# Six row loads for the third attention, issued one a tile early in the routed experts instead of together near their end

## The chip, the cores and the metric

One Trainium2 chip, one core of it. The metric is the device time of one launch in microseconds, as the median of several executions. In the profile PE is TensorE, PEld its weight loads, DVE VectorE, ACT ScalarE, POOL GpSimd, SP SyncE; SPq and POOLq are the queues on which SP and POOL issue DMAs.

## What is computed

A batch of 32 sequences of 128 rows by 256 features goes through two attentions against the context and two feed-forward blocks, each on the layer-normed input with a residual added:

```python
x = x + _L0_xattn_ref(_layernorm(x, axis=-1), ctx_1024, ctx_1024)      # 16 heads
x = x + _L0_ffn_ref(_layernorm(x, axis=-1), ...)                        # 8 experts, top 2, plus a shared one
x = x + _L1_xattn_ref(_layernorm(x, axis=-1), ctx_1024, ...)            # c2q and q2c attention, 4*D -> D
x = x + _L1_ffn_ref(_layernorm(x, axis=-1), ...)                        # butterfly, gelu, butterfly
```

The part around the change is the second line. In it each row is sent to two of eight experts:

```python
h = jnp.einsum('bsd,edh->bseh', x, W1) * jax.nn.silu(jnp.einsum('bsd,edh->bseh', x, W3))
expert_out = jnp.einsum('bseh,ehd->bsed', h, W2)
out = jnp.einsum('bsed,bse->bsd', expert_out, w_full)
out = out + jnp.einsum('bsh,hd->bsd', hs, Ws2)
```

## The kernel before

The kernel runs in blocks, one after the other with a barrier of all engines between them: the first attention (to about 230 us of the trace), the shared expert with routing (to about 383), the routed experts (to about 711), the "third attention" (the reference's third line, to about 890) and the last feed-forward. There is no scheduler: each engine has its own program, a Python loop over tiles whose order is written out by hand, and waits on semaphores.

**Shared expert.** In pairs p of sequences the sum of the residual and the shared expert's output is stored from `ao` to `acc_d` in HBM (L708, semaphores `s_ast`). POOL scatters the normed rows, sorted by expert, to `xs_d`.

**Routed experts.** The sorted rows are worked through in NE = 71 tiles of 128 rows, t = 0 to 70. For a tile PE multiplies its turned rows `xT` with the expert's weights W3 into `Ge` and W1 into `Ue`, six matmuls each; ACT makes `sg` of `Ge`, DVE makes `he` of both. `he` has to be turned before it meets W2. In tiles 0 to 31 and in the last two PE turns it (L1075). In tiles 32 to 68 (`by_dma`) ACT and DVE split it into two halves `hs` (L1145, L1183), and a transposing DMA on SP's queue writes `hT` (L1048). PE's product `Ye` of tile t - 2 comes at the end of loop step t (L1082 is the line of all three products, in a helper). DVE scales it to `ye`, and SP stores that to `ys_d`.

**SP's queue.** It does this in step t, in this order: load `xe` for tile t + 4 (once PE has turned tile t), transpose tile t in the `by_dma` tiles (once `hs` is there), store `ye` of tile t - 2. In step 8 seven small loads come first (`small_weights`, L1027 to L1030). In step NE - 6 = 65 six loads of 256 KB come first: `ax` (the stored `acc_d`, L1039) and `cx` (the context, L1040) for the pairs 0, 1 and 2 of the third attention, behind a wait for all stores of `acc_d`. `ax` and `cx` have buffers of their own, which nobody writes or reads before.

**POOL** multiplies out the butterflies of the last block beside it, with loads of 1 MB (`bw`, L1232).

**Third attention.** POOL gathers each row's two expert outputs from `ys_d` (L1414) once all `ye` are stored. DVE adds them to `ax`, norms the sum, and PE turns it (`Tc`, L1762) and the context (`Tq` from `cx`, L1765). The pairs from 3 on are loaded in that block (L1388, L1392), with waits on pairs three before.

Of the kernel before, what the change touches and what calls it, by code (L numbers as in the profile page):

```python
# [56 lines left out]
def build_program(nc, x, ctx_in, Wr, rb, W1, W2, W3, Ws1, Ws2, Ws3, w_cq, b_cq, w_c, b_c, w_q, b_q,  # L57
# [12 lines left out]
    NE = (NB * TOPK * P + E * (P - 1)) // P  # L70
# [8 lines left out]
    def dram(name, shape, dt=F32):  # L79
        return nc.dram_tensor(name, shape, dt, kind="Internal").ap()  # L80
# [4 lines left out]
    acc_d = dram("acc_d", (NB, P, D))  # L85
# [4 lines left out]
    with ctx:  # L90
# [874 lines left out]
        ax = per("ax", [P, 3, 2, D])  # L965
        cx = per("cx", [P, 3, 2, D])
        s_w5, s_b5 = sem("s_w5"), sem("s_b5")
        s_ax, s_cx = sems("s_ax", 3), sems("s_cx", 3)
# [6 lines left out]
        with ExitStack() as ph:  # L975
# [24 lines left out]
            pair = lambda a, p: a[2 * p:2 * p + 2, :, :].rearrange("t p n -> p t n")  # L1000
# [17 lines left out]
            with nc.Block() as block:  # L1018
                @block.sync
                def _(sp):  # L1020
                    as_col = lambda a: a.rearrange("(c p) -> p c", p=P)
                    as_rows = lambda a, n: a.rearrange("(o d) -> o d", o=1).broadcast_to([P, n])

                    def small_weights():

                        for i, w in enumerate((w_cq, w_q, w_c)):
                            sp.dma_start(wcq[:, i, :], as_col(w), allow_slow_non_contiguous=True).then_inc(s_w5, 16)  # L1027
                        sp.dma_start(blb[:, :], as_rows(b_l, D)).then_inc(s_w5, 16)
                        for i, b in enumerate((b_cq, b_c, b_q)):
                            sp.dma_start(bias3[:, i:i + 1], as_rows(b, 1)).then_inc(s_w5, 16)  # L1030

                    for t in range(-2, NE + 2):
                        if t == 8:
                            small_weights()
                        if t == NE - 6:
                            for j in range(2):
                                sp.wait_ge(s_ast[j], 16 * (NP // 2))
                            for p in range(3):
                                sp.dma_start(ax[:, p, :, :], pair(acc_d, p)).then_inc(s_ax[p], 16)  # L1039
                                sp.dma_start(cx[:, p, :, :], pair(ctx_in, p)).then_inc(s_cx[p], 16)  # L1040
                        if t + 4 < NE:
                            if t >= 2:
                                sp.wait_ge(s_xt, t + 1)
                            sp.dma_start(xe[:, t % 4, :], xs_d[(t + 4) * P:(t + 5) * P, :]).then_inc(s_xe[t % 4], 16)
                        if by_dma(t):
                            sp.wait_ge(s_hl4, BASE_L + t + 1)
                            sp.wait_ge(s_ye, t - 2)
                            sp.dma_start_transpose(hT[:, t % 3, :, :, :].rearrange("p l c n -> p (l c) n"),  # L1048
                                                   hs[:, t % 2, :, :].rearrange("p l n -> p (l n)")).then_inc(s_hT[t % 2], 16)
                        if t >= 2:  # L1050
                            sp.wait_ge(s_yc, t - 1)
                            sp.dma_start(ys_d[(t - 2) * P:(t - 1) * P, :], ye[:, t % 2, :]).then_inc(s_yst[t % 2], 16)
# [278 lines left out]
        with ExitStack() as ph:  # L1331
# [48 lines left out]
            pair = lambda a, p: a[2 * p:2 * p + 2, :, :].rearrange("t p n -> p t n")  # L1380
# [656 lines left out]
```

## Time and profile before

| | |
|---|---|
| median of 3 runs | 1049.26 us (1045.29 to 1050.29) |
| span of the profiled execution | 1070.0 us |
| PE busy | 977.7 us (91%) |
| DVE busy | 708.4 us (66%) |
| ACT, POOL busy | 558.5 us, 558.9 us (52% each) |
| SP's DMA queue (q1) | 111.60 MB, 35.8% of 16 engines |

Of the profiled execution only the span is known, no time of its own beside it; its span is 20.7 us above the median of the runs. PE's busy share says little by itself, since stages with different limits are put together in it. The granted clock (PEclk) is 1.00 at 2.4 GHz and 0.50 at 1.2 GHz.

### The profile page before, as it was taken

To read this page: it belongs to the slowest core of one execution; us is meant where nothing else is said; L and a number is where in the kernel's file an instruction comes from. 1 tells how busy PE (TensorE), PEld (TensorE's weight loads), DVE (VectorE), ACT (ScalarE), POOL (GpSimd) and SP (SyncE) were. 2 spreads that over 40 slices of the span, in tenths; PEclk is the share of its full clock that TensorE was granted. 3 is DMA by queue.
4 is the path that set the end of the run, shared out by engine and by line. 5 is a ranking of instruction groups with operands and counts; after the bars stand their busy time and mean duration, and the time that the engine had idled before them with its cause. 6 is when DMAs were issued, how large, how long until landed. Compare 5 with 4: busy or idle time off the path is not lost. (4 is left out here: it accounts for less than half of the span.)

```text
span 1070.0 us, 27041 instructions
## 1 busy us (share of the span) xinstructions
PE 977.7 (91%) x9282; PEld 757.6 (71%) x9282; DVE 708.4 (66%) x1682; ACT 558.5 (52%) x1140; POOL 558.9 (52%) x737
## 2 busy tenths in 40 slices
PE   5999999767699989999999999877999998999998
PEld 3666666556388856666666666546989997989897
DVE  6999999756366734445455555457888975565653
ACT  5999999723154523333323333335445546667664
POOL 6777777204544549999999990227556501000000
PEclk9999999979699999999999999988999999999999
DMA  5455444346599874555445555724454302211110
GB/s 147 156 163 161 151 155 141 100 153 197 180 296 318 284 212 155 187 174 177 139 93 121 122 117 118 177 79 129 127 155 142 120 31 70 61 41 60 39 50 30
DMA packets 153161, 147.90 MB, mean 138 GB/s; under 512 B 51440, under 2 KB 141776, under 8 KB 151248
## 3 DMA queue, kind: packets, MB, share of 16 engines
q1 hardware_dynamic: 143808, 111.60, 35.8%
q0 software_dynamic: 9232, 34.67, 9.8%
q8 instruction: 78, 1.28, 0.5%
q14 instruction: 43, 0.35, 0.1%
HBM read 84.22 MB, written 52.30 MB: 128 GB/s over the span
## 5 line engine op out<-in xcount | busy, mean ns | idle before, releaser
L941 POOL DMA_INDIRECT xs_d<-ht,slot x64 | 67.0, 1048 | 86.5 <-DMA ht<-h_d 40.3
L1082 PE MATMUL Ye<-wm,hT 128*128 x852 | 105.9, 274 | 2.7 <-DMA hT<-hs 2.5
L1082 PE MATMUL Ge<-wm,xT 128*128 x426 | 104.3, 381 | 2.1 <-issue 1.0
L1082 PE MATMUL Ue<-wm,xT 128*128 x426 | 103.5, 379 | 0.0
L1082 PEld LDWEIGHTS Ye<-wm,hT 128*128 128x128 f16 x852 | 83.6, 98 | 27.3 <-issue 3.5
L1943 ACT ACTIVATE gf<-H,bup,wdesc 128x256 f32<-128x256 f32 x128 | 71.8, 563 | 54.1 <-DVE g L1916 33.9
L1972 PE MATMUL H<-T6s,wm 128*128 128x256 f16 x768 | 94.0, 273 | 2.7 <-PEq L1381 1.6
L1984 PE MATMUL Y<-wm,g 128*128 128x256 f16 x768 | 93.8, 273 | 1.5 <-DVE g L1916 1.5
L1414 POOL DMA_INDIRECT yg<-ys_d,slot x64 | 66.8, 1044 | 51.8 <-DMA ys_d<-ye 34.4
L1916 DVE SCALAR_TENSOR_TENSOR g<-gf,g 128x512 f16<-128x512 f32 x64 | 44.7, 698 | 71.0 <-ACT g L1948 71.0
L1150 ACT ACTIVATE sg<-Ge 128x512 f32<-128x512 f32 x71 | 42.4, 597 | 82.8 <-PE Ge L1082 82.8
L350 DVE TENSOR_REDUCE nmx<-S 128x8 bf16<-128x1024 f32 x64 | 78.4, 1224 | 9.9 <-PE S L532 7.1
L1972 PEld LDWEIGHTS H<-T6s,wm 128*128 128x128 f16 x768 | 75.0, 98 | 12.0 <-issue 1.9
L1984 PEld LDWEIGHTS Y<-wm,g 128*128 128x128 f16 x768 | 75.0, 98 | 10.5 <-DVE g L1916 2.1
L1187 DVE SCALAR_TENSOR_TENSOR xT<-XB,xT 128x256 f16<-128x256 f32 x71 | 30.1, 424 | 71.8 <-ACT xT L1156 71.8
L1082 PEld LDWEIGHTS Ge<-wm,xT 128*128 128x128 f16 x426 | 41.9, 98 | 38.0 <-issue 3.9
L1856 POOL TENSOR_TENSOR rs<-mv,epsc 128x2 f32<-128x2 f32 x14 | 3.2, 226 | 125.3 <-DVE mv L1880 125.3
L429 ACT ACTIVATE pT<-ST 128x1024 f32<-128x1024 f32 x64 | 68.0, 1062 | 1.0 <-PE ST L564 0.9
L1082 PEld LDWEIGHTS Ue<-wm,xT 128*128 128x128 f16 x426 | 41.7, 98 | 34.5
L1140 ACT CAST hT<-HT 128x512 f16<-128x512 f32 x34 | 19.9, 585 | 80.8 <-PE HT L1075 80.8
L1194 DVE SCALAR_TENSOR_TENSOR he<-Ue,sg 128x512 f32<-128x512 f32 x71 | 49.1, 691 | 17.6 <-PE Ue L1082 17.6
L1205 DVE TENSOR_SCALAR ye<-Ye 128x256 f32<-128x256 f32 x71 | 30.1, 425 | 43.8 <-PE Ye L1082 42.8
(291 smaller groups left out, 2497.2 us busy)
## 6 DMA issues: line engine op xcount, KB each, us to landing
stage<-in_L_ffn_W_dram SPq DMA_DIRECT2D x24, 512.0 KB
xs_d<-zeros SPq DMA_DIRECT2D x36, 256.0 KB, 2.6
ys_d<-ye SPq DMA_DIRECT2D x71, 128.0 KB, 2.1
xe<-xs_d SPq DMA_DIRECT2D x69, 128.0 KB, 2.4
bw<-in_L_ffn_up_weights_dram POOLq DMA_DIRECT2D x7, 1024.0 KB, 5.7
bw<-_L_ffn_down_weights_dram POOLq DMA_DIRECT2D x7, 1024.0 KB, 5.6
xb<-in_x_dram SPq DMA_DIRECT2D x32, 128.0 KB, 2.4
cb<-in_ctx_dram SPq DMA_DIRECT2D x32, 128.0 KB, 3.1
```

The lines of the kernel that those rows point to most:

```text
L350: V.tensor_reduce(nmx[:, h, :, 0:HP2], S[:, :, :, :], AX.X, ALU.max, negate=True).then_inc(s_mx, 1)
L429: A.activation(pT[:, h, :, :, :], ST[:, :, :, :], ACT.Exp, scale=DH ** -0.5).then_inc(s_exp, 1)
L941: nc.gpsimd.indirect_dma_start(out=xs_d[:, :], out_offset=bass.IndirectOffsetOnAxis(ap=slot[:, j, 2 * t + i:2 * t + i + 1], axis=0), in_=h ...
L1082: last = nc.tensor.matmul(bank, left[:, xp, c, :], wm[:, kind, bass.ds(e, 1), wp, c * width:(c + 1) * width], start=i == 0 and c == 0, sto ...
L1150: nc.scalar.activation(sg4[:, t % 2, :], Ge[t % 2][:, :], ACT.Silu, scale=1 / (XS * WS)).then_inc(s_sl4, 1)
L1187: STT(xT[:, (t + 1) % 2, LO, :, :], XT, XS, xT[:, (t + 1) % 2, HI, :, :], ALU.mult, ALU.subtract).then_inc(s_xte, 1)
L1194: STT(he[:, t % 2, :], Ue[t % 2][:, :], ES / (XS * WS), sg4[:, t % 2, :], ALU.mult, ALU.mult).then_inc(s_he, 1)
L1414: nc.gpsimd.indirect_dma_start(out=yg[:, p % 2, j, k, :], out_offset=None, in_=ys_d[:, :], in_offset=bass.IndirectOffsetOnAxis(ap=slot[:, ...
L1916: nc.vector.scalar_tensor_tensor(g6[:, k % 2, LO, 2 * q:2 * q + 2, :], gf[:, q, :, :], GS, g6[:, k % 2, HI, 2 * q:2 * q + 2, :], ALU.mult, ...
L1943: nc.scalar.activation(gf[:, q, j, :], H6[b % 4][:, :], ACT.Gelu, bias=bup[:, b:b + 1], scale=wdesc[:, 0:1]).then_inc(s_g6, 1)
L1972: last = nc.tensor.matmul(H6[b % 4][:, :], wup[:, c, wp, b * P:(b + 1) * P], T6s[k % 2][:, xp, c, :, :], start=i == 0 and c == 0, stop=i = ...
L1984: last = nc.tensor.matmul(Y6[j][:, :], g6[:, k % 2, xp, half * FC // 2 + b, j * P:(j + 1) * P], wdp[:, half, wp, b * D:(b + 1) * D], start ...
```

## The change

The six loads leave step 65. The wait for the stores of `acc_d` is made in step 10, and the loads follow one a step: `ax` of the pairs 0, 1 and 2 in steps 10, 11 and 12, `cx` of the same pairs in steps 13, 14 and 15. Buffers, semaphores and contents are the same.

```diff
-                        if t == NE - 6:
+                        if t == 10:
                             for j in range(2):
                                 sp.wait_ge(s_ast[j], 16 * (NP // 2))
-                            for p in range(3):
-                                sp.dma_start(ax[:, p, :, :], pair(acc_d, p)).then_inc(s_ax[p], 16)
-                                sp.dma_start(cx[:, p, :, :], pair(ctx_in, p)).then_inc(s_cx[p], 16)
+                        if 10 <= t < 13:
+                            sp.dma_start(ax[:, t - 10, :, :], pair(acc_d, t - 10)).then_inc(s_ax[t - 10], 16)
+                        if 13 <= t < 16:
+                            sp.dma_start(cx[:, t - 13, :, :], pair(ctx_in, t - 13)).then_inc(s_cx[t - 13], 16)
```

SP's queue around step 65, before. `xe` is the load of tile 69's rows, `hT<-hs` the transpose of tile 65 (`s_ot` counts its halves, `s_ye` the products), `ys_d<-ye` the store of tile 63:

```order
L1052 DMA ys_d<-ye 128x256 [waits s_yc]
L1039 DMA ax<-acc_d 128x2x256 [waits s_ast1,s_ast0]
L1040 DMA cx<-in_ctx_dram 128x2x256
L1039 DMA ax<-acc_d 128x2x256
L1040 DMA cx<-in_ctx_dram 128x2x256
L1039 DMA ax<-acc_d 128x2x256
L1040 DMA cx<-in_ctx_dram 128x2x256
L1044 DMA xe<-xs_d 128x256 [waits s_xt]
L1048 DMA_TRANSPOSE hT<-hs 128x8x128 [waits s_ye,s_ot]
L1052 DMA ys_d<-ye 128x256 [waits s_yc]
```

The six stood ahead of the load and the transpose of step 65; now the steps 64 and 65 follow each other like all others (the lines are one higher in the changed kernel).

SP's queue in steps 9 to 14, as it is now; there are no transposes in these tiles:

```order
L1045 DMA xe<-xs_d 128x256 [waits s_xt]
L1053 DMA ys_d<-ye 128x256 [waits s_yc]
L1039 DMA ax<-acc_d 128x2x256 [waits s_ast1,s_ast0]
L1045 DMA xe<-xs_d 128x256 [waits s_xt]
L1053 DMA ys_d<-ye 128x256 [waits s_yc]
L1039 DMA ax<-acc_d 128x2x256
L1045 DMA xe<-xs_d 128x256 [waits s_xt]
L1053 DMA ys_d<-ye 128x256 [waits s_yc]
L1039 DMA ax<-acc_d 128x2x256
L1045 DMA xe<-xs_d 128x256 [waits s_xt]
L1053 DMA ys_d<-ye 128x256 [waits s_yc]
L1041 DMA cx<-in_ctx_dram 128x2x256
```

Each of the six stands alone between the store of one step and the load of the next, and the wait for `s_ast` stands behind the store of step 9. The other engines' programs are unchanged.

## Rows read from the trace of the kernel before

**Rows 1.** The page: busy time, share of the span, instructions.

```profile
PE 977.7 (91%) x9282; PEld 757.6 (71%) x9282; DVE 708.4 (66%) x1682; ACT 558.5 (52%) x1140; POOL 558.9 (52%) x737
```

**Rows 2.** Windows: length, busy (count) of PE, PEld, DVE, ACT, POOL; PEclk, DMA share, GB/s.

```profile
431.00:454.00 23.00, 23.00 (x153) 15.28 (x152) 11.16 (x20) 7.51 (x16) 22.14 (x18) 1.00 0.50 180
683.00:693.00 10.00, 7.46 (x46) 4.23 (x43) 4.28 (x8) 3.07 (x7) 0.00 (x0) 1.00 0.95 252
639.00:682.00 43.00, 42.66 (x269) 26.60 (x267) 23.89 (x42) 15.62 (x32) 9.34 (x21) 1.00 0.59 126
713.00:736.00 23.00, 11.30 (x54) 8.51 (x54) 16.20 (x41) 11.49 (x24) 18.08 (x20) 0.63 0.35 104
736.00:759.00 23.00, 22.48 (x140) 20.43 (x141) 20.09 (x79) 12.77 (x42) 14.63 (x17) 1.00 0.46 138
```

**Rows 3.** Timeline of PE around step 67: start us, length us, instructions [idle before <-releaser].

```profile
681.87 1.47 PE L1082 MATMUL Ye<-wm,hT 128*128 x12
...
685.98 1.47 PE L1082 MATMUL Ye<-wm,hT 128*128 x12
687.29 1.46 PE L1082 MATMUL Ge<-wm,xT 128*128 x6
...
688.81 1.46 PE L1082 MATMUL Ue<-wm,xT 128*128 x6
692.81 1.61 PE L1082 MATMUL Ye<-wm,hT 128*128 x12 [2.54 <-DMA hT<-hs]
694.61 1.47 PE L1082 MATMUL Ge<-wm,xT 128*128 x6 [0.20 <-issue]
```

**Rows 4.** Timeline of SP's queue in steps 64 and 65.

```profile
680.31 2.19 SPq L1048 DMA_TRANSPOSE hT<-hs  x1
...
683.23 0.38 SPq L1039 DMA_DIRECT2D ax<-acc_d  x1
...
685.74 0.47 SPq L1040 DMA_DIRECT2D cx<-in_ctx_dram  x1
...
686.81 2.28 SPq L1048 DMA_TRANSPOSE hT<-hs  x1
```

**Rows 5.** Timeline of DVE: the second half of tile 65's `hs`.

```profile
683.72 0.68 DVE L1183 TENSOR_TENSOR hs<-he,hs 128x512 f16<-128x512 f32 x1
```

**Rows 6.** Line L1048, all 37 transposes: issue time, who waited, time to landing.

```profile
L1048 SPq DMA_TRANSPOSE hT<-hs x37: 1237/1239/2276, 537.8 to 700.0; - x37
...
  PE Ye L1082: 2.5, 1
...
DMA to landing us min/median/max: 3.0/3.1/5.9
```

**Rows 7.** Timeline of SP's queue: the last `acc_d` store, and steps 8 to 10.

```profile
382.69 0.37 SPq L708 DMA_DIRECT2D acc_d<-ao  x1
...
422.01 1.34 SPq L1027 DMA_DIRECT2D wcq<-in_L_xattn_w_cq_dram  x1
...
426.83 0.43 SPq L1052 DMA_DIRECT2D ys_d<-ye  x1
...
430.76 0.32 SPq L1052 DMA_DIRECT2D ys_d<-ye  x1
431.13 0.43 SPq L1044 DMA_DIRECT2D xe<-xs_d  x1
435.32 0.32 SPq L1052 DMA_DIRECT2D ys_d<-ye  x1
```

**Rows 8.** Line L1044, the 61 loads of `xe` between 400 and 683 us.

```profile
DMA to landing us min/median/max: 2.1/2.4/8.3
```

**Rows 9.** Timeline of POOL: the first gather of the third attention.

```profile
713.35 1.19 POOL L1414 DMA_INDIRECT yg<-ys_d,slot  x1 [34.44 <-DMA ys_d<-ye]
```

**Rows 10.** Windows, PE alone: length, PE busy (count), PEclk, DMA share, GB/s.

```profile
715.00:716.00 1.00, 0.48 (x3) 0.69 0.50 131
...
732.00:733.00 1.00, 0.70 (x2) 0.78 0.02 4
```

## The prediction

> **What bounds the kernel now.** I read the page first: PE is busy for 977.7 us of a span of 1070.0 us [rows 1]. That is an average over blocks, so it is no answer yet for the place of the change. The table of windows is, because it separates stretches. In 431 to 454 us, where the loads go to, PE has no idle time at all (23.00 of 23.00), with the DMA engines half busy. In 639 to 682 us, shortly before the place they leave, it works 42.66 of 43.00 us at full clock. In 683 to 693 us it works only 7.46 of 10.00, and the DMA share is 0.95 there against 0.59 before [rows 2]. So the routed experts are bound by PE, and what changes the time there is what makes PE idle.
>
> The timeline of PE shows how it idles. The product `Ye` that starts at 692.81 has 2.54 us of idle time before it, and what ended the wait is the transposing DMA `hT<-hs` [rows 3]. The line of the transposes says it once more: of 37 transposes a single one made PE wait, 2.5 us, and while the median lands 3.1 us after its issue, the slowest took 5.9 [rows 6]. The timeline of SP's queue says why this one was late. The first of the six loads is issued at 683.23 and the last at 685.74, and the transpose follows at 686.81 [rows 4], although its input was complete at 683.72 + 0.68 = 684.40 [rows 5]. It was issued 2.41 us late, and then took 5.9 - 3.1 = 2.8 us longer than the median, with 1.5 MB of the six loads ahead of it.
>
> **What leaves step 65.** Without the six issues the transpose of tile 65 goes out at about 684.45, as tile 64's did at 680.31. It lands 3.1 us later, at 687.55. PE wants it when `Ue`, begun at 688.81, has been issued. Undisturbed, `Ye` starts 685.98 - 681.87 = 4.11 us after the `Ye` before it [rows 3], so it is wanted at 690.09: 2.5 us of slack, against a landing of 686.81 + 5.9 = 692.71 before. The wait goes entirely. Nothing else of the step becomes late: the load of `xe` is for four tiles on, and the store of `ye` frees a buffer two tiles on.
>
> The price of the wait is more than its 2.54 us. The `Ge` behind it starts at 694.61, the `Ge` before it at 687.29 [rows 3]: 7.32 us where an undisturbed step takes 4.11, so 3.21 us were lost. The difference to 2.54 is the first products after the wait (1.61 against 1.47 us, a gap of 0.20, and the overlap with the product before that is lost). I take 3.2 us for the term. Its bounds: it can't be below 0 from this side, since a load removed ahead of the transpose delays nobody, and the most that the two rows allow is 3.2 us.
>
> **What passes it on.** The loss stands 19 us before the block's end, in an unbroken chain on PE. The next block's first gather waits for the last `ye` to be stored and starts at 713.35, after 34.44 us of waiting [rows 9]; it depends on PE's last product and on nothing that keeps its own time. POOL has been idle for most of those 34 us, so it isn't late either. I see nothing that would absorb the 3.2 us up to the kernel's end, where the last block runs on PE.
>
> **What arrives in steps 10 to 15.** The wait for the `acc_d` stores costs nothing: the last of them was issued at 382.69, and step 10 comes after 431 us [rows 7]. Each load costs SP one issue, 0.47 us [rows 4]. It is put ahead of the `xe` load, and behind that SP sits idle in each step, from 431.13 + 0.43 to the next store at 435.32: 3.76 us of idle time for 0.47 [rows 7]. In steps 10 to 15 there is no transpose whose delay PE could feel. The best evidence is in the trace itself: seven loads in a row were issued in step 8 from 422.01, and put the store of that step at 426.83; by 431.13 SP was back in its rhythm, and PE has no idle time anywhere in the window that follows [rows 2, 7]. What hides the transfers is that `xe` is loaded four tiles (over 16 us) ahead, and its slowest landing in all of the block was 8.3 us [rows 8]. 256 KB more in a step adds 262144 B / 4.56 us = 57 GB/s to the 180 GB/s of that stretch [rows 2], where a step is 435.32 - 430.76 = 4.56 us long [rows 7]; the stretch around the burst moved 252. If that cover were gone, a step would wait for its rows, which PE's idle time would show at once. I cost this part at 0, which the full PE beside the seven loads of step 8 speaks for. The bounds are 0, since nothing here can gain, and +1.1 us: two of the six loads at a full sixth of what the burst cost, 2 x 3.2 / 6.
>
> At the third attention nothing changes: `ax` and `cx` for the pairs 0 to 2 were there in time before, and PE's first wait there is for normed rows.
>
> **A rule that speaks against it.** The stretch of the burst moved 252 GB/s [rows 2], at which 6 x 262144 B = 1.57 MB need 6.2 us, until 689.5: the transpose of 686.81 met a queue that was still full, and its 5.9 us agree. The Trainium skill (DMA: Bandwidth & Descriptors, Specifications) gives a fabric ceiling of 435 GB/s; at that the burst would be gone after 3.6 us, at 686.8, the transpose would land undisturbed at 689.9, just before 690.1, and by that figure an estimate of the wait is nil and so is the gain. The trace, with 252 GB/s and a wait of 2.54 us, doesn't agree with it here.
>
> **The sum.** -3.2 + 0 = -3.2 us on the profiled span: 1070.0 becomes 1066.8. The span is 20.7 us above the runs' median. I found no reason for the wait to be different in an undisturbed run, as it comes from the order on SP's queue, so I subtract the same from the median: 1049.26 - 3.2 = 1046.1 us, or -0.3%. From here on, "no change" is within 0.5%, 5.2 us, about what a measurement of this kernel can tell from no change: 1044.0 to 1054.5.
>
> **Rivals.**
> 1. *The wait isn't the burst's.* Some landing would be slow anyway at this place, or in unprofiled runs the burst hides. For it: two more transposes had long issues (2.19 us for tile 64's, with no loads before it [rows 4]). Against: one in 37 made PE wait, and it is the one behind the six loads [rows 6]. Time 1049.3. Chance 0.08.
> 2. *Given back in steps 10 to 15.* The loads meet the 1 MB loads of `bw`, whose products PE needs later, or `xe`. It would cost up to what the burst did, so the time is 1047 to 1049. Against: a full PE with half of the DMA share free [rows 2]. Chance 0.07.
> 3. *The clock, to the slow side.* The granted clock falls to 0.50 in 715 to 716 us and is back in 732 to 733 [rows 10]: 17 us at 1.2 GHz around the start of the third attention, where PE mostly waits (11.30 of 23.00 us busy). Right behind, PE is busy for 22.48 of 23.00 us [rows 2]. All of this comes 3.2 us earlier now. If the clock comes back later relative to the work, each us of it costs up to half a us; it decides against the change from about 6.5 us of delay, and another stretch as long as this one would cost 17 x 0.5 x 22.48 / 23.00 = 8.3 us, giving 1049.26 - 3.2 + 8.3 = 1054.4. For it: nothing holds the clock's fall to a place in the program. Against: what PE does before the fall stays the same. The Trainium skill (TensorE: Matmul & The Clock Gate, Part 1) says that the gate looks at activity in periods that run on by themselves and don't begin with the kernel; that the fall would move against the work is by that rule, and no run here shows it yet. Chance 0.07 in all, some 0.04 of it above 1054.5 together with scatter.
> 4. *The clock, to the fast side.* The same shift can make the low stretch shorter or leave it to idle time. In 713 to 736 us the 11.30 us of PE at a mean clock of 0.63 would be 11.30 x 0.63 = 7.1 us at full clock, 4.2 less [rows 2]; if three quarters of that are waited for, 3 us more are gained, so 1043. Chance 0.10.
> 5. *The change does nothing it says.* The order on SP's queue shows that it does; left out.
>
> **How the numbers follow.** My forecast, -3.2 us with nothing given back, has 0.68. With three runs before, which reach from 1045.29 to 1050.29, the medians compared scatter by some 2 us, and that, not the mechanism, makes most of the range: 1046.1 - 3.6 = 1042.5 below, which takes in the fast clock and the scatter; 1050.0 above, which takes in rivals 1 and 2. Some 2 in 10 is left out, beyond the clock's cases. Faster by over 0.5% needs 1044.0 or less: from the forecast with 2 us of favourable scatter (about 0.15 of 0.68) and from half of rival 4, together 0.16. Slower by over 0.5%: 0.04. No change: 0.80.
>
> **What would show it.** Right: no PE wait for `hT<-hs` in the whole block, and the slowest transpose landing in under 4 us; the transpose of tile 65 issued right behind its `hs`; `Ge` steps of 4.11 us from tile 60 to 68; PE's busy time in the routed experts unchanged; steps 10 to 15 still at 4.56 us with PE never idle; the distance from the block's first product to the first gather down by 3.2 us. Wrong: a PE wait elsewhere in the block, `ye` waiting for its store, a POOL wait for `bw`, or a low clock that lasts beyond 20 us after the block's end.

## The result, and the profile after

| | before | with the change |
|---|---|---|
| median of 22 runs | 1049.45 us (1045.29 to 1054.78) | 1046.14 us (1042.80 to 1049.68) |
| ratio, 95% interval | | 0.997 (0.9957 to 0.9982) |
| span of the profiled execution | 1070.0 us | 1043.8 us |
| PE busy | 977.7 us (91%) | 965.4 us (92%) |

The change takes 3.3 us off, the interval being 1.9 to 4.5 us. The forecast was 3.2 us. The two spans differ by far more, 26.2 us, and that isn't the change: 23.64 us of it lie ahead of the first product of the routed experts (385.46 against 361.82 us), in blocks that the change doesn't touch. The profiled execution of the kernel before had a slow stretch there: between 265 and 290 us, in the same products of the shared expert, PE is busy for 14.29 us at a mean granted clock of 0.63, against 25.00 us at 1.00. The pauses between its products have no cause that the profile shows, and none of the 22 runs is as long as this execution. The windows of before and of the changed kernel, columns as in [rows 2]:

```profile
265.00:290.00 25.00, 14.29 (x61) 6.67 (x60) 5.07 (x7) 2.78 (x6) 15.66 (x16) 0.63 0.61 206
265.00:290.00 25.00, 25.00 (x231) 22.40 (x230) 19.74 (x28) 14.09 (x21) 19.52 (x19) 1.00 1.04 372
```

Another 1.2 us lie behind the first gather of the third attention, from which it is 356.65 us to the end before and 355.44 now. So the two traces are compared within the block.

The line of the transposes in the changed kernel, answering [rows 6]:

```profile
L1049 SPq DMA_TRANSPOSE hT<-hs x37: 1232/1233/2350, 513.4 to 675.0; - x37
...
  PE Ye L1083: 2.1, 2
DMA to landing us min/median/max: 3.0/3.1/5.0
```

The slowest landing fell from 5.9 to 5.0 us. But PE still waits for transposes, twice, 2.1 us in sum. Neither is the old one. The timeline of PE around step 67, answering [rows 3]:

```profile
668.31 1.47 PE L1083 MATMUL Ye<-wm,hT 128*128 x12
669.62 1.46 PE L1083 MATMUL Ge<-wm,xT 128*128 x6
```

No idle time stands at this `Ye` of step 67 or at any other of the steps 63 to 70, and the transpose of tile 65 goes out 0.03 us after its `hs`. The two waits are earlier:

```profile
647.03 1.66 PE L1083 MATMUL Ye<-wm,hT 128*128 x12 [1.05 <-DMA hT<-hs]
648.88 1.47 PE L1083 MATMUL Ge<-wm,xT 128*128 x6 [0.19 <-issue]
```

That is step 62; the other is in step 52. SP's queue in steps 10 and 11, where the first loads went, answering [rows 7]:

```profile
407.12 0.32 SPq L1053 DMA_DIRECT2D ys_d<-ye  x1
407.55 0.37 SPq L1039 DMA_DIRECT2D ax<-acc_d  x1
407.96 0.54 SPq L1045 DMA_DIRECT2D xe<-xs_d  x1
411.68 0.32 SPq L1053 DMA_DIRECT2D ys_d<-ye  x1
412.04 0.44 SPq L1039 DMA_DIRECT2D ax<-acc_d  x1
412.52 0.48 SPq L1045 DMA_DIRECT2D xe<-xs_d  x1
```

The store comes every 411.68 - 407.12 = 4.56 us, as before. The windows of the changed kernel, answering [rows 2] (length; busy of PE, PEld, DVE, ACT, POOL; PEclk, DMA share, GB/s):

```profile
407.00:430.00 23.00, 23.00 (x153) 15.28 (x152) 11.25 (x21) 7.41 (x16) 22.20 (x17) 1.00 0.70 233
657.00:667.00 10.00, 10.00 (x63) 6.14 (x62) 5.30 (x10) 3.40 (x8) 0.00 (x0) 1.00 0.67 131
```

In steps 10 to 15 the traffic went from 180 to 233 GB/s, 53 of the 57 that were worked out, and PE stays at 23.00 of 23.00 us. In the ten microseconds around step 65 PE has no idle time, where it had 2.54 us.

The starts of the steps' `Ge` products measure the whole block. These are the distances from one to the next, for the only steps in which the executions differ by more than 0.2 us, worked out from the starts in the timelines of PE. The last two columns are executions of experiments below: the change a second time, and the change with cut maxima.

| from step to step | before | change | change again | with cut maxima | undisturbed |
|---|---|---|---|---|---|
| 0 to 1 | 4.33 | 4.33 | 4.33 | 6.01 | 4.33 |
| 34 to 35 | 7.72 | 7.54 | 8.50 | 5.81 | - |
| 35 to 36 | 5.68 | 4.98 | 5.44 | 4.99 | 4.98 |
| 42 to 43 | 4.12 | 4.41 | 4.12 | 4.12 | 4.12 |
| 52 to 53 | 4.78 | 5.84 | 4.62 | 4.12 | 4.12 |
| 62 to 63 | 4.62 | 5.87 | 6.06 | 4.12 | 4.12 |
| 67 to 68 | 7.32 | 4.13 | 4.12 | 4.12 | 4.12 |

The row of step 67 holds the effect: 7.32 - 4.13 = 3.19 us. In this pair of executions steps 52 and 62 give back 1.06 + 1.25 us, and so the block, from the first product to the third attention's first gather, is not 3.2 us shorter, as was forecast for it, but only (713.35 - 385.46) - (688.36 - 361.82) = 1.35 us shorter. The rows add up to it: -3.19 + 1.06 + 1.25 - 0.70 - 0.18 + 0.29 is -1.47, and 0.12 us more are lost in step 66. The second execution of the change shows step 52 at 4.62: the waits of steps 52 and 62 vary by themselves. The rows of step 0 and of step 34 vary too, together and with no edit behind them (about 6.0 and 5.8 us in e1, e4, e7 and e10), so they are no part of any effect. Part of it is the granted clock: it is 0.50 for some 3 us within step 0 in those four executions, and around the steps 34 and 35 in before, e2, e3, e5, e9 and e11. Step 34 also waits for POOL's `bdiag`. One window of each kind, first e10, then before (PE alone: length, PE busy, PEclk, DMA share, GB/s):

```profile
364.00:366.00 2.00, 2.00 (x8) 0.50 0.86 268
545.00:547.00 2.00, 2.00 (x10) 0.50 0.00 0
```

### The profile page after: what moved, and what is told of

It is laid out like the page before. It is cut to its first block and busy times, and to the rows that moved or that the text cites. A ratio compares the mean times of both kernels' runs of the same rounds, so it can differ in the third digit from the quotient of the medians.

```text
span 1043.8 us, 27041 instructions
## 1 busy us (share of the span) xinstructions
PE 965.4 (92%) x9282; PEld 754.9 (72%) x9282; DVE 709.3 (68%) x1682; ACT 559.2 (54%) x1140; POOL 560.8 (54%) x737
## 5 line engine op out<-in xcount | busy, mean ns | idle before, releaser
L941 POOL DMA_INDIRECT xs_d<-ht,slot x64 | 70.2, 1097 | 58.4 <-DVE slot L857 30.2
```

The costliest lines, as they stand in the source:

```text
L941: nc.gpsimd.indirect_dma_start(out=xs_d[:, :], out_offset=bass.IndirectOffsetOnAxis(ap=slot[:, j, 2 * t + i:2 * t + i + 1], axis=0), in_=h ...
```

## The experiments

Each has the time of its runs and their ratio to the kernel before, measured beside it on the same chip. The medians of before were 1049.62 us beside e1 to e4, 1050.39 beside e5 to e7, and 1048.99 beside e8 to e11.

**e1: the same six together, but early.**

```diff
-                        if t == NE - 6:
+                        if t == 10:
```

> All six loads together again, but in step 10. My theory (the wait came of a late and slowed transpose that PE needed soon; in steps 10 to 15 no transpose runs on the queue, and the loads of xe have four tiles of lead): no PE wait in steps 8 to 20, time as with the change, 1046.1 us or a ratio near 0.997. Rival (what helps is the spreading, a burst costs PE about 3 us wherever it stands): some PE or DVE wait behind step 10 and a ratio near 1.000.

1045.68 us, ratio 0.9962 (0.9946 to 0.9978). The burst was there, six issues from 409.44 to 412.77 us, and the stretch behind it moved 288 GB/s, more than the 252 of the old place [rows 2]:

```profile
403.00:409.00 6.00, 6.00 (x44) 4.29 (x43) 3.11 (x6) 1.46 (x3) 5.69 (x5) 1.00 0.61 157
409.00:415.00 6.00, 6.00 (x39) 3.87 (x38) 2.93 (x5) 2.19 (x5) 5.61 (x6) 1.00 0.95 288
```

PE loses nothing beside it. The gain is from the place; one a tile is no better than all at once there. The landings of `xe` between 400 and 430 us went up to a median of 4.0 and a maximum of 7.1 us (3.2 and 5.6 with the change), which its lead of four tiles covers.

**e2: one a step, but late.** The change's lines with steps 62 to 67 in place of 10 to 15:

```diff
-                        if t == 10:
+                        if t == NE - 9:
-                        if 10 <= t < 13:
+                        if NE - 9 <= t < NE - 6:
-                        if 13 <= t < 16:
+                        if NE - 6 <= t < NE - 3:
```

> One load a step, but late: steps 62 to 67, with transposes on the queue. My theory (slack of 2.5 us before PE needs a transpose; one load makes it some 0.5 us late and some 0.5 us slower): no PE wait for hT in steps 62 to 68, landings under 4 us, ratio near 0.997. Rival (bytes beside a transpose cost PE their share, 0.5 us each): six small waits, 3 us in sum, ratio near 1.000.

1046.37 us, ratio 0.9962 (0.9942 to 0.9982). PE waited in steps 52 and 62 (1.01 and 0.90 us), in no later step. One landing between 650 and 680 us took 4.9 us, not under 4 as I had written, and PE still didn't wait. So spreading alone is enough too. Either half of the edit gives all of the gain, as far as the intervals can tell.

**e3: the six behind the transpose of their step.**

```diff
-                        if t == NE - 6:
-                            ...
                             sp.dma_start(ys_d[(t - 2) * P:(t - 1) * P, :], ye[:, t % 2, :]).then_inc(s_yst[t % 2], 16)
+                        if t == NE - 6:
+                            ...
```

> The six loads in step 65 as before, but behind the transpose and the store of that step. My theory: the transpose of tile 65 lands in time; SP's queue gets through the six issues some 3 us later, so the transpose of tile 66 is the late one (issued about 1 to 1.5 us after its hs, and slowed to 5 to 6 us): a wait of 1 to 2 us moves one step on, ratio about 0.998 to 1.000. Rival 1 (only the order on the queue counts): no wait, ratio 0.997. Rival 2 (only the bytes count): the same 2.5 us wait one step later, ratio 1.000.

1049.01 us, ratio 0.999 (0.9971 to 1.0008): by the medians most of the gain is lost, by the trace some 2 of the 3.2 us. The next transpose was the victim. From the timeline, DVE's `hs` and SP's queue:

```profile
666.89 0.39 SPq L1051 DMA_DIRECT2D ax<-acc_d  x1
...
668.34 0.68 DVE L1183 TENSOR_TENSOR hs<-he,hs 128x512 f16<-128x512 f32 x1
...
670.48 2.33 SPq L1042 DMA_TRANSPOSE hT<-hs  x1
...
676.38 1.59 PE L1082 MATMUL Ye<-wm,hT 128*128 x12 [1.37 <-DMA hT<-hs]
```

It was ready at 669.02, issued 1.46 us late, and took 5.8 us to land. 1.46 + 5.8 - 3.1 = 4.2 us, less the slack of about 2.5, leaves 1.7 against a wait of 1.37. That is the middle case of the three expected. The step became 6.09 - 4.12 = 1.97 us longer, 0.6 more than its wait, as in the kernel before.

**e5: half the dose.** `ax` together in step 65, `cx` one a step in 13 to 15.

```diff
-                        if t == 10:
+                        if t == NE - 6:
                             for j in range(2):
                                 sp.wait_ge(s_ast[j], 16 * (NP // 2))
-                        if 10 <= t < 13:
-                            sp.dma_start(ax[:, t - 10, :, :], pair(acc_d, t - 10)).then_inc(s_ax[t - 10], 16)
+                            for p in range(3):
+                                sp.dma_start(ax[:, p, :, :], pair(acc_d, p)).then_inc(s_ax[p], 16)
```

> Half the dose: the three ax loads together at the head of step 65, the three cx loads one a step in steps 13 to 15. My theory (slack of 2.5 us): the transpose is issued about 0.9 to 1.2 us late and lands about 1.4 us slower, together about the slack, so a PE wait of 0 to 0.5 us, not half of 2.54. Rival (cost in proportion to the bytes): a wait of 1.3 us, 1.6 us in all.

1046.75 us, ratio 0.9968 (0.9945 to 0.9991). The timeline of DVE and SP:

```profile
664.11 0.68 DVE L1184 TENSOR_TENSOR hs<-he,hs 128x512 f16<-128x512 f32 x1
...
665.37 1.23 SPq L1049 DMA_TRANSPOSE hT<-hs  x1
```

The transpose was 665.37 - 664.79 = 0.58 us late and landed 3.9 us after its issue: 1.4 us against a slack of 2.5, and PE did not wait. What is left is 0.36 us in step 66 (4.48 us for 4.12), where the changed kernel has 0.12 as well; the transpose of tile 64 landed after 4.9 us in both. A price in proportion to the bytes would have left a wait of 1.3 us. The wait has a threshold.

**e6 and e8: SP's queue held up, with next to no bytes.** Both are the change plus six small loads into an unused buffer at the head of step 65. e6:

```diff
+                        if t == NE - 6:
+                            for i in range(6):
+                                sp.dma_start(tiny[:, i:i + 1], as_rows(b_q, 1)).then_inc(s_tiny, 16)
```

> The change, and six loads of 512 bytes each at the head of step 65, so that SP's queue is held up as before but next to no bytes are moved. My theory (lateness 2.4 us alone is just under the slack of 2.5 us): transpose issued 2.2 to 2.6 us late, landing 3.1 to 3.5 us, PE wait 0 to 0.5 us. Rival (the queue order alone makes the wait): PE wait near 2.5 us. Rival (the bytes alone): 0, and the run below shows 2.5.

1050.65 us, ratio 1.0011 (0.9992 to 1.003). The rival seemed to win: a wait of 3.8 us, longer than the one of 1.5 MB.

```profile
669.81 2.24 PE L1088 MATMUL Ye<-wm,hT 128*128 x12 [3.77 <-DMA hT<-hs]
```

But the windows show what these loads did (columns as above):

```profile
661.00:663.00 2.00, 2.00 (x17) 1.42 (x15) 1.12 (x2) 0.58 (x3) 0.00 (x0) 1.00 0.06 0
663.00:665.00 2.00, 2.00 (x13) 1.08 (x11) 1.02 (x2) 0.80 (x2) 0.00 (x0) 1.00 0.05 0
665.00:667.00 2.00, 1.03 (x5) 0.29 (x3) 1.12 (x2) 0.43 (x2) 0.00 (x0) 1.00 0.06 0
667.00:669.00 2.00, 0.00 (x0) 0.00 (x0) 0.00 (x0) 0.00 (x0) 0.00 (x0) 1.00 0.81 194
```

For six microseconds the mean share of 16 DMA engines is 0.05 to 0.06 at 0 GB/s: next to nothing but the 128 x 6 pieces of 4 bytes is under way, and the load and the transpose behind them on the queue wait. I took the share for one engine busy all the time (see the expectation of e8). The share doesn't tell this from sixteen engines busy for a sixteenth of it each, so how many work is not shown. The transpose issued at 662.86, 2.69 us late, landed 6.8 us later. Step 67 became 8.78 us long, 4.66 more than undisturbed, and step 68 1.04 more, beyond a wait of 3.77, since the granted clock fell behind this wait, as behind no other wait for `hT` (PE alone, columns as before):

```profile
671.00:672.00 1.00, 1.00 (x6) 0.50 0.04 11
```

So e6 holds up the queue's transfers and not only its issue, and doesn't test what it was made for. e8 has six loads of 16 rows of 64 bytes instead:

```diff
+                                sp.dma_start(tiny[0:16, 16 * i:16 * i + 16], b_l.rearrange("(p d) -> p d", d=16)).then_inc(s_tiny, 16)
```

> The change, and at the head of step 65 six loads of 1 KB each (16 rows of 64 bytes, so all 16 DMA engines get one short row of each) in place of the 4-byte loads of the earlier run, which kept a single DMA engine busy for 8 us (DMA share 0.05 to 0.06, 0 GB/s) and so were no test of the issue alone. My theory (lateness alone, 2.4 us, stays under the slack of 2.5 us): the transpose is issued 2.2 to 2.7 us late and lands within 3.5 us of it, PE wait 0 to 0.7 us, ratio 0.997 to 0.998. Rival (the place in SP's queue alone makes the wait, however few bytes): PE wait of 2 us or more, ratio near 1.000.

1046.49 us, ratio 0.9974 (0.9958 to 0.9991). SP's queue and DVE:

```profile
660.34 2.75 SPq L1045 DMA_DIRECT2D tiny<-in_L_xattn_b_l_dram  x6
661.34 0.68 DVE L1189 TENSOR_TENSOR hs<-he,hs 128x512 f16<-128x512 f32 x1
663.13 0.42 SPq L1049 DMA_DIRECT2D xe<-xs_d  x1
663.60 1.47 PE L1088 MATMUL Ye<-wm,hT 128*128 x12
663.65 1.23 SPq L1053 DMA_TRANSPOSE hT<-hs  x1
```

The transpose was issued 663.65 - 662.02 = 1.63 us late (less than the 2.41 of the kernel before, since SP came to step 65 earlier), landed in 3.2 us, and PE had no wait after step 62. Lateness of this size alone costs nothing. A lateness of 2.41 us alone was not had, so that point stays an estimate.

**e7: the bytes, with SP's queue free.** GpSimd issues the six at the time of step 65, without the wait for the stores of `acc_d`; their consumers wait on a semaphore of their own.

```diff
+                    pool.wait_ge(s_xt, NE - 5)
+                    for p in range(3):
+                        pool.dma_start(ax[:, p, :, :], pair(acc_d, p)).then_inc(s_bx, 16)
+                        pool.dma_start(cx[:, p, :, :], pair(ctx_in, p)).then_inc(s_bx, 16)
```

> The six loads at the time of step 65, but issued by GpSimd, whose queue is idle there, so that SP's queue is free. My theory: the transpose of tile 65 goes out within 0.2 us of its hs and is slowed by the bytes to at most 5.9 us, which leaves a PE wait of 0 to 0.5 us there or at tile 66. Rival (the bytes alone make the wait): a wait near 2.5 us.

```profile
656.35 0.68 DVE L1178 TENSOR_TENSOR hs<-he,hs 128x512 f16<-128x512 f32 x1
656.81 0.73 POOL L1318 DMA_DIRECT2D cx<-in_ctx_dram  x1
657.05 1.24 SPq L1043 DMA_TRANSPOSE hT<-hs  x1
...
664.01 1.66 PE L1077 MATMUL Ye<-wm,hT 128*128 x12 [1.11 <-DMA hT<-hs]
```

This is tile 64's transpose, of the step before: GpSimd was free a little earlier than SP would have been, and it is step 66 that waited. The transpose went out 0.02 us after its input was ready and landed 6.8 us later, 3.7 more than the median. Against a slack of 2.5 that leaves 1.2, and PE waited 1.11 us. So the bytes alone do cause a wait, more than the 0 to 0.5 us I had written, since they slowed the transpose by 3.7 and not by at most 2.8 us; but less than half of the old one; with what follows it the step became 5.90 - 4.12 = 1.78 us longer, over half of the old loss. The time, 1051.60 us, ratio 1.0017 (0.9995 to 1.0039), isn't explained by that wait. The profiled execution was the fastest of this kernel's ten, 1045.24 us, and where the others spent 6 us more no trace shows. It stays open; the reading of this run rests on the trace alone.

**e4, e10, e11: the waits in steps 52 and 62.** `he` of step 50 and of step 60 is followed on VectorE by a maximum over a folded weight matrix. The timeline of DVE in the changed kernel, around the first of them:

```profile
596.53 2.28 DVE L1174 TENSOR_REDUCE wmax<-wdn 128x1 f32<-128x2048 f32 x1
598.72 0.70 DVE L1184 TENSOR_TENSOR hs<-he,hs 128x512 f16<-128x512 f32 x1
...
601.04 0.72 DVE L1184 TENSOR_TENSOR hs<-he,hs 128x512 f16<-128x512 f32 x1 [0.31 <-ACT hs L1146]
```

The reduction stands where the `hs` of tile 50 would have been made, which so starts at 598.72, 2.2 us late; the next `hs` comes 2.3 us behind it in place of 4.1. PE waited for the transpose of tile 50, the first of the two, and not for the second, as I had expected for e4. It was issued at 599.45 and landed after 4.5 us: 2.2 us of late input and 1.4 us of slow landing are 3.6 us against the slack, and the wait was 1.04 us. The transpose right behind the reduction landed after 4.4 to 4.8 us in all eleven cases in which PE waited in step 52 or 62, and after 3.0 or 3.1 us in all nine in which it didn't. So the whole reduction takes most of the slack each time, and a slow landing, in some, takes more than the rest. Why it is slow in some is not shown.

The edit cuts the reductions in four, over successive steps, and begins the second in step 56 instead of 60:

```diff
-            FOLD_UP, FOLD_DN, LATE = 34, 46, 60
+            FOLD_UP, FOLD_DN, LATE = 34, 46, 56
-                        nc.vector.tensor_reduce(wmax[:, i:i + 1], w[:, :, 0:D], AX.XY, ALU.max,
-                                                apply_absolute_value=True).then_inc(s_bv, 1)
+                        if k < 4:
+                            nc.vector.tensor_reduce(wpart[:, i, k:k + 1], w[:, 2 * k:2 * k + 2, 0:D], AX.XY, ALU.max,
+                                                    apply_absolute_value=True).then_inc(s_wpart, 1)
+                        else:
+                            dve.wait_ge(s_wpart, 4 * (2 - i))
+                            nc.vector.tensor_reduce(wmax[:, i:i + 1], wpart[:, i, :], AX.X, ALU.max).then_inc(s_bv, 1)
```

> The change, and the two maxima over the folded weights (one VectorE reduction of 2.28 us each, in steps 50 and 60) cut into four reductions of some 0.6 us in successive steps (50 to 53, 56 to 59) and a small one behind. In the trace after the change PE waits 2 x 1.05 us for transposes right behind these reductions, and loses about 1.75 us at each with what follows. Theory (the reduction delays hs, two transposes then follow closely and the second lands late): both waits gone, block 2 to 3.5 us shorter, time 1043 to 1045 us, ratio 0.994 to 0.996. Rival (the landing is slow there by chance, or the pieces delay VectorE's chain in nine steps instead): waits stay or move, ratio 0.997.

1045.18 us, ratio 0.995 (0.9932 to 0.9968), no PE wait for `hT`. As its interval overlaps that of the change, it was run again beside the change, and alone on the kernel before.

> The change once more, beside the next two on the same chip. Both theories: ratio 0.996 to 0.998. Its trace tells whether the two waits of 1.05 us behind the maxima come in every execution or in some.

> The change with the cut maxima once more. Theory (each whole maximum delays two transposes and costs PE up to 1.75 us in a part of the executions, which the cut ends): 1 to 2 us under the change run beside it, ratio 0.994 to 0.996, no PE wait for hT. Rival (the difference seen was scatter): the same as the change beside it within 0.5 us.

> The kernel before, with the cut maxima alone. Theory (both effects are separate waits of PE and add up): the wait of 2.5 us in step 67 stays, the others are gone, ratio 0.998 to 0.999. Rival (PE time gained earlier in the block is lost again, or the cut maxima alone do all of it): ratio 1.000, or 0.995.

| beside each other | median | ratio to before, 95% interval |
|---|---|---|
| e9, the change again | 1047.15 us | 0.9979 (0.9961 to 0.9997) |
| e11, cut maxima alone | 1048.19 us | 0.9983 (0.9968 to 0.9999) |
| e10, both | 1043.58 us | 0.9945 (0.9925 to 0.9966) |

The two effects are separate: (1 - 0.9979) + (1 - 0.9983) = 0.0038, and both together give 0.0055, the same within the intervals. The traces agree. e10 has cut reductions of 0.68 us:

```profile
L1176 DVE TENSOR_REDUCE wpart<-wdn x4: 674/675/677, 597.0 to 609.4; 128x1 f32<-128x512 f32 x4
```

and all its steps from 36 to 68 at 4.11, 4.12 or, with a product of the folding, 4.98 or 4.99 us (table above). e4 shows the account at work: the transpose of tile 50 landed after 4.4 us there too, but its input was only 0.6 us late, and PE did not wait. e11 has only the wait that the change removes, and 0.73 us lost in step 59 without a wait, where the transpose landed after 4.9 us:

```profile
669.49 1.59 PE L1083 MATMUL Ye<-wm,hT 128*128 x12 [2.15 <-DMA hT<-hs]
```

In the change's own two executions the waits are there twice and once:

```profile
648.10 1.66 PE L1083 MATMUL Ye<-wm,hT 128*128 x12 [1.26 <-DMA hT<-hs]
```

Of the ten executions with whole maxima six have PE waits for `hT` in step 52 or 62 (the change, e2, e3, e5 and e8 in both, e9 in one). Four have none there (before, e1, e6, e7), though something is lost there in them too: their step 52 is still 4.70 to 4.80 us long. The three with cut maxima have none, and steps of 4.12 to 4.50 us at both places.

The version with both is the fastest that was run, 0.5% under the kernel before. Its median is 3.6 us under that of the change beside it on the same chip, and e4's was 1.0 us under the change's first measurement. So it is likely faster than the change alone, by an amount that stays uncertain.

## Why the prediction was right

**The term of 3.2 us.** In the trace it is 3.19 us, the distance from the `Ge` of step 67 to that of step 68. The medians give 3.3, with 1.9 to 4.5. The working took the loss from the restart of the chain and not from the idle time of 2.54 us, and the table shows that this was right: the first product after a wait and the gap behind it belong to its price. The medians can't tell 3.2 from 2.5, so this rests on the steps. e11's wait of 2.15 us makes its step 6.88 - 4.12 = 2.76 us longer, again 0.6 more than the wait.

That 3.3 came so near to 3.2 is in part luck. I had found no reason for the wait to be different in another execution, and e11, with the same burst, lost 2.76. Of the 2.41 us of lateness 0.95 were not the burst's: the transpose of tile 64, with no load ahead, took 2.19 us to issue instead of 1.24 and pushed the six loads back. In e11 it took 1.24 (but the store behind it 1.06 instead of 0.58 us), and the transpose of tile 65 was 1.94 us late; in e3 the lateness was 1.46. With 2.41 - 0.95 = 1.46 us the wait would be about 1.6 us and the loss 2.2, an estimate from these rows.

**The threshold.** I had put the transpose's delay together from 2.41 us of late issue and 2.8 us of slow landing, against 2.5 us of slack. Seven doses now lie on that account: 1.4 us of delay gives no wait (e5), 1.63 + 0.1 none (e8), 3.7 gives 1.11 (e7), 4.2 gives 1.37 (e3), 1.94 + 2.8 gives 2.15 (e11), 5.2 gave 2.54, and 2.69 + 3.7 gives 3.77 (e6). Each wait is the delay less some 2.6 to 2.8 us. Of the kernel before, either part alone, 2.41 or 2.8 us, is near what the slack takes, and the wait is mostly their sum. In e7 the bytes alone took more, 3.7 us.

The same holds for every transpose. `Ye` starts 2.81 us after its step's `Ge` if it needn't wait. In the steps 44 to 68 of all 13 executions 16 transposes landed after that time, and PE waited for the overshoot each time, within 0.15 us. Where one landed 0.2 to 0.9 us ahead of it there was no wait, but the step was up to 0.7 us longer all the same. Further ahead nothing was lost, but for 0.15 us in step 51 of e2 and e5 and for the step of e6 that the low clock made longer. So the loss begins before the wait does, at a delay of about 1.8 us.

**Steps 10 to 15 at no cost.** Right: 23.00 of 23.00 us of PE, and even all six together cost nothing there (e1).

**The hand-over to the end.** The third attention begins as much earlier as the block ends. In this pair neither clock rival shows: the granted clock drops and returns at the same points of the work. In the changed kernel (windows with PE alone: length, PE busy, PEclk, DMA share, GB/s):

```profile
690.00:691.00 1.00, 0.48 (x3) 0.88 0.45 131
...
707.00:708.00 1.00, 0.81 (x2) 0.59 0.01 4
```

The first gather is at 688.36, so the return to 2.4 GHz comes within 18.6 to 19.6 us of it; before, it was 732 to 733 against 713.35 [rows 9, 10], 18.7 to 19.7. The rule that the gate's periods run by themselves (the Trainium skill, TensorE: Matmul & The Clock Gate, Part 1) would have allowed a shift; in this pair of executions none is seen beyond the microsecond of the windows. In others one is. In the second execution of the change (e9) the clock falls in 689 to 690 us, right at the first gather of 689.26, and is back in 709 to 710:

```profile
689.00:690.00 1.00, 0.00 (x0) 0.73 0.00 0
709.00:710.00 1.00, 0.97 (x5) 0.53 0.38 115
```

That is some 20 us at 1.2 GHz instead of 17, and from the gather to the end it took 356.5 us against 355.4 in the change's first execution. e1 has the longer stretch too, the other eleven have 17 us. So the slow side of the clock rival exists, at about 1 us; whether the change makes it more frequent, so few executions can't show.

**What was wrong in it.** I had written that there would be no PE wait for `hT` in the whole block and no landing above 4 us. The trace has two waits and a landing of 5.0 us. I had read one execution of before, in which the steps 52 and 62 were 0.66 and 0.50 us too long and no row showed a wait for `hT`, and took 37 transposes with one slow one as the rule. The reduction on VectorE takes 2.2 us of the slack there in each execution that has it whole, just short of a wait, and a landing of 4.4 to 4.8 us, in some, goes beyond. Both kernels have the reduction, so I see no effect on the forecast of the difference, but that the waits come equally often in both is not shown: the kernel before has one trace. The reading of one execution hid a further gain, and the same waits are why two more signs failed: `Ge` steps of 4.11 us from tile 60 to 68, and a block shorter by 3.2 us in the traces. The rival that something other than the burst made PE wait got 0.08 and was wrong for step 67, but such waits exist elsewhere in the block.

The estimate from the fabric ceiling (the Trainium skill, DMA: Bandwidth & Descriptors, Specifications), by which the burst would be gone in time and the gain nil, doesn't fit: the time fell by 3.3 us, the stretches around the burst moved 252 and, in e1, 288 GB/s, and e7 shows the transpose slowed by 3.7 us with SP's queue free.

## What to carry to other kernels

A small transfer on whose arrival the bound engine depends has a slack, and it is worth working out: the wait is lateness at the queue plus slowness in the transfer, less that slack. The loss is some 0.6 us more than the wait, and it begins a little before the wait does. Bulk loads with no hurry belong where the queue carries nothing of the kind, or one at a time; either will do. And where one such wait is found, the other things that eat the same slack (here a 2.3 us reduction ahead of the transpose's input) should be looked for in more than one execution.

## What was unexpected

Six loads of a broadcast scalar, 128 pieces of 4 bytes each, 3 KB in all, delayed the transpose behind them more than 1.5 MB in full rows did: 6.8 against 5.9 us to landing, with next to nothing moved meanwhile (DMA share 0.05 to 0.06, 0 GB/s). The same count of loads as 16 rows of 64 bytes delayed it by 0.1 us. The kernel itself has three such scalar loads in step 8, where no transpose follows them.

The issue of a transpose on SP, 1.24 us as a rule, took 2.28 us behind the burst [rows 4] and 2.33 in e3; the longest, 3.50 us, stood behind the scalar loads of e6:

```profile
665.29 3.50 SPq L1053 DMA_TRANSPOSE hT<-hs  x1
```

But 2.19 us also occur with no load ahead [rows 4], so a long issue by itself isn't proof of a full queue.
